# A Mamba block with a mixture of experts on one core: the next chunk's front part moved one unit sooner

## The reference

```
xz = u @ in_proj_w.T;  x_in, z = split(xz, 2)          # 256 channels each
xc = silu(causal_conv4(x_in) + conv_b)
dt, Bm, Cm = split(xc @ x_proj_w.T, [8, 24])
delta = softplus(dt @ dt_w.T + dt_b)
dA  = exp(delta * A)                                   # 16 states n for each channel
dBu = delta * Bm * xc
h = dA_t * h + dBu_t;   y = sum_n h * C_t              # over the time steps
y = (y + xc * D) * silu(z);  x = x + y @ out_w.T
# then x + silu(gate) * val @ ffp_w.T, then + sum over the top 2 of 8 experts
```

## Time and profile before

| | us |
|---|---|
| median of 3 runs | 856.88 |
| lowest and highest | 855.81, 859.95 |
| the profiled execution | 856.53 |
| its span from first to last instruction | 854.7 |
| DVE busy | 744.2 |
| PE busy | 655.0 |
| POOL busy | 583.4 |
| ACT busy | 498.0 |

### The profile page before, as it was taken

One profiled execution on the slowest core, in us unless ns is written; L12 is line 12 of the kernel. 1 busy time (PEld: TensorE's weight loads), 2 busy tenths in 40 slices (PEclk: granted clock), 3 DMA queues, 4 the chain that ended last, 5 costly groups with the idle time before them and its releaser, 6 DMA issues.

```text
span 854.7 us, 12652 instructions
## 1 busy us (share of the span) xinstructions
PE 655.0 (77%) x3573; PEld 472.6 (55%) x3573; DVE 744.2 (87%) x1147; ACT 498.0 (58%) x1071; POOL 583.4 (68%) x487
## 2 busy tenths in 40 slices
PE   4538688888677787897788687887785689987991
PEld 2224454455355446773477446763584457787991
DVE  1286999999999999999999999999999987785675
ACT  2545796876778576555756576556743664432440
POOL 1085676777966896788958985789758973455452
PEclk9659899999979988997989997997886689997996
DMA  7823234223313336543553246432635320122248
GB/s 177 268 89 102 87 112 124 77 82 117 113 55 101 100 103 203 151 125 94 179 160 131 97 116 206 129 109 99 187 108 164 126 86 20 45 57 70 61 126 236
DMA packets 81785, 102.31 MB, mean 120 GB/s; under 512 B 10344, under 2 KB 48948, under 8 KB 81700
## 3 DMA queue, kind: packets, MB, share of 16 engines
q1 hardware_dynamic: 77395, 92.58, 36.3%
q0 software_dynamic: 4320, 8.92, 2.9%
HBM read 89.93 MB, written 15.35 MB: 123 GB/s over the span
## 4 chain that ended last, share of the span: by engine, by line
DVE 36%; PE 33%; issue 19%; ACT 7%; SPq 2%; DMA 2%; POOL 1%; DVEq 1%; ACTq 0%; POOLq 0%
DVE state L1059 19%; DVE product L1069 5%; PE y L1270 4%; PE work_front L1230 3%; PE up L1383 2%; PE gate L1376 2%; PE y L1266 2%; PE up L1394 2%; PE work_front L1236 2%; DVE stats L989 2%; ACT decay L923 2%; PE gate L1295 1%; SPq L701 1%; PE up L1295 1%; DVE arena L1034 1%
## 5 line engine op out<-in xcount | busy, mean ns | idle before, releaser
L800 POOL TENSOR_TENSOR inflow<-du,b_wide 128x1024 f32<-128x1024 f32 x128 | 315.4, 2468 | 143.7 <-DVE product L1069 94.2
L1059 DVE TENSOR_TENSOR_SCAN state<-decay,carry,inflow 128x512 f32<-128x512 f32 x192 | 234.7, 1264 | 6.2 <-ACT decay L923 5.4
L1069 DVE TENSOR_TENSOR product<-state,c_wide 128x1024 f32<-128x1024 f32 (+1 forms) x98 | 149.8, 1528 | 3.7 <-PE y L1266 2.5
L1266 PE MATMUL y<-ident,product 128*128 128x128 f32 x704 | 111.9, 304 | 33.6 <-DVE product L1069 33.5
L1266 PEld LDWEIGHTS y<-ident,product 128*128 128x128 f32 x704 | 92.2, 158 | 76.3 <-DVE product L1069 41.1
L923 ACT ACTIVATE decay<-delta_odd,a_neg 128x512 f32<-128x512 f32 x128 | 86.5, 688 | 66.7 <-DVE state L1059 65.6
L830 POOL DMA_INDIRECT y_dram<-y_rows,x_rows x71 | 82.7, 1165 | 58.9 <-ACT y_rows L979 51.5
L923 ACT ACTIVATE decay<-arena,a_neg 128x512 f32<-128x512 f32 x128 | 86.3, 687 | 56.9 <-DVE state L1059 50.0
L1270 PE MATMUL y<-h_rows,ident 128*128 128x512 f32 x160 | 90.7, 660 | 7.7 <-ACT h_rows L888 7.1
L824 POOL DMA_INDIRECT row_dram<-m_tok,place x64 | 73.9, 1154 | 24.2 <-issue 14.3
L1059 DVE TENSOR_TENSOR_SCAN state<-decay,inflow 128x512 f32<-128x512 f32 x64 | 74.4, 1202 | 5.7 <-POOL inflow L800 2.5
(11 more groups left out here) (234 smaller groups left out, 1323.6 us busy)
## 6 DMA issues: line engine op xcount, KB each, us to landing
b_wide<-bc_dram SPq DMA_DIRECT2D x128, 256.0 KB
c_wide<-bc_dram SPq DMA_DIRECT2D x98, 256.0 KB
w_stage<-gate_up_dram SPq DMA_DIRECT2D x29, 344.0 KB, 4.3
x_rows<-row_dram SPq DMA_DIRECT2D x71, 65.0 KB, 2.9
arena<-gate_up_dram SPq DMA_DIRECT2D x8, 344.0 KB
x_tok<-in_x SPq DMA_DIRECT2D x8, 256.0 KB, 6.1
out<-x_tok SPq DMA_DIRECT2D x8, 256.0 KB
inflow<-y_dram SPq DMA_DIRECT2D x6, 256.0 KB, 3.1
```

Of the source, the lines that this page charges most:

```text
L800: e.tensor_tensor(inflow[:, key % 3], du[:, c % 2], b_wide[:, key % ROW_SLOTS:key % ROW_SLOTS + 1, :].to_broadcast([P, HALVES, CHUNK]), AL ...
L1059: e.tensor_tensor_scan(state[:, key % STATE_SLOTS, h, :], decay_bank[h][:], inflow[:, key % 3, h, :], 0.0 if c % (SEQ // CHUNK) == 0 else ...
L1069: e.tensor_tensor(product[:, key % 2, :, :wide], state[:, key % STATE_SLOTS, :, :wide], c_wide[:, key % ROW_SLOTS:key % ROW_SLOTS + 1, :wi ...
L1266: t = e.matmul(y_bank[r][:, y_at(s, h)], product[:, key % 2, h, s * P:(s + 1) * P], ident[:], is_transpose=True, start=n == 0 and s % 2 + ...
```

## The change

Two numbers in `plan`. A second front row is taken in unit 4 of chunk 0 too, so every later row comes one unit sooner; and the rows of the chunk after the next begin at unit 12, not 13. Before, rows 0, 1, 2 of the list run in units 13, 14, 15 and row 3 in unit 0 of the next chunk; now rows 0 to 3 run in units 12 to 15. Row 3 holds `u_tok`, `u_turn`, `u_t`, `halo` and `in0a`. `log_dt` goes from unit 9 to unit 8, and `series`, `small`, `log1p` from unit 10 to 9. No instruction is added or taken away.

```diff
-EARLY_FRONT = (1, 2, 3)
+EARLY_FRONT = (1, 2, 3, 4)
@@
         if i in EARLY_FRONT:
             put_all(*take_front(c + 1, 1))
-        front = take_front(c + (1 if n < D_STATE - 3 else 2), 1)
+        front = take_front(c + (1 if n < D_STATE - 4 else 2), 1)
         if n == 0 and c:
```

## The result

| | before | after |
|---|---|---|
| median, us | 856.55 of 4 runs | 875.20 of 4 runs |
| lowest and highest | 855.81, 859.95 | 873.13, 878.71 |
| the profiled execution | 856.53 | 878.71 |
| its span | 854.7 | 876.9 |

The ratio of after to before is 1.0214, with a 95% interval of 1.0181 to 1.0246: 18.65 us slower by the medians, where 14.1 over the median was forecast. The profiled execution of after is the highest of its four and 3.5 us over their median. So what it shows is partly what this one execution did. Its mean granted clock of TensorE (0.859) isn't lower than that of the other three (0.858, 0.853, 0.851); where its 3.5 us come from isn't shown.

The account below looks back on a forecast made before the run. The prediction took DVE to bound the unit loop, busy 71.1 of 74.4 us. It summed 856.5 + 11.1 (passages) + 3.3 (port), nothing for the softplus, to 870.9, said 871.0, with 860 to 881 to hold 8 in 10.

Parts of the forecast that it names:

- not more than 2 us each: Sign of error: stretches of the later chunks, without such a passage, moving by more than 2 us each.
- The chain, 13.4: Ends of chunks 0, 1, 2: ACT and PE steps from unit 14's scan end to `y_gate` sum to 13.4 us.
- S: End of unit 14's scan; taken to shift by -0.2 us in chunk 0 and -0.7 each in chunks 1 and 2.
- 5.7, 3.5 and 3.5: How much later, in us, `y_gate` comes after S at the ends of chunks 0, 1 and 2.
- Rival C: Slower: at the passages PE idles, then runs `in0a` and the totals at low clock; 881 us, chance 0.17.
- Part 2: Port between DVE and POOL: moved DVE steps meet or escape POOL's `inflow`; +3.3 us in sum.
- The 1.5 that it took off: Units 14 and 15, three chunks: `picked` finds POOL free (-0.8), the choice meets an `inflow` (+0.3); -1.5 us.
- the lock on the port: Unit 14, chunks 1 and 2: by the skill's exclusive lock the second choice step is held up 2.2; sum 0.7 more.
- Part 3: Softplus on ACT: `log_dt`, moved from unit 9 to 8, holds the next decays back by 4.8 but stays covered; nothing taken.
- 11.1, 3.3 and 0: Forecast terms in us: passages out of chunks 0 to 2, port between DVE and POOL, softplus on ACT.
- a DVE operation with two operands in SBUF: At the DVE/POOL port: such an operation that meets an `inflow` waits for its end.

## Why the prediction was right, and where it was off

**The mechanism and its place were right.** DVE waits ahead of `y_gate` at the ends of chunks 0, 1 and 2 and at no later one, for the sums of L1270, with L1230 ahead of them, and putting the crossing row back takes all but 0.2 of these waits and 11.8 us away. The stretches of the later chunks moved by 1.2, 1.3, 0.8, 1.4 and -2.0, about the "not more than 2 us each" that was asked.

**The chain, 13.4.** In the profile of after it is 16.9, 16.9 and 14.3, and as a reading of that profile the term is too small by 3.5, 3.5 and 0.9. The first passage shows why. Over the sum come the two waits of ACT for the turns (0.74 + 1.72) and the longer `in0a` (3.66 - 1.98 = 1.68). Off it comes 0.85: the sum had 1.98 for both totals ahead of `y_gate`, which began 1.13 after them (131.75 against 130.62). That is 3.3 of the 3.5. With the full clock, in the run with `rstd3` sooner, ACT waits only 0.44, and 13.4 + 0.44 - 0.85 = 13.0 is the distance there; the 3.9 between the two is the low clock. So the sum was right within 0.4 for the clock that it assumed, with two small errors that partly cancel, and `u_turn` hides beside the decays there but for the 0.44. The forecast should have given the chain two prices and a chance to each, instead of one price and a rival.

Measured by itself the crossing costs 12.8 ± 3.7 us against 12.7, and that the two agree so closely is luck. DVE alone doesn't need 9.9 after S at the second and third passages but 11.6: `picked` is held up as before, and a second routing step now is as well. By the trace the crossing added 6.8, 2.4 and 2.7 and not 5.7, 3.5 and 3.5.

**Rival C** came in part: in the profiled execution of after `in0a` ran at the low clock at the first two passages and not at the third (1.98). The Trainium skill (page TensorE: Matmul & The Clock Gate, Part 1) has an idle TensorE go back to 1.2 GHz. The traces agree in that the low clock of the first passage comes behind 2.51 us of idle time, and they add that the same 2.5 us, ahead of the same instruction, ended once in the low clock and once not.

**S.** Taken as 1.6 sooner over three chunks. In chunk 0 S is 0.2 later (114.87 against 114.69), though the first scan began 1.3 earlier in this execution (45.5 against 46.8), so 1.5; from `y_gate` to the next S it is 0.5 longer and 1.1 shorter. That is 0.9 later in all, so this term was off by 2.5. The gain in units 12 and 13 came in both chunks, by 2.4 and 3.0. What the sum lacked is what stands ahead of them: from `y_gate` to the end of unit 11 chunks 1 and 2 are 2.9 and 2.0 longer, 1.15 of it the held-up shift of unit 11 in each.

**Part 2, the port, +3.3.** The hold-up of the shift is there (1.27, forecast "about 1.3"), and it was counted for chunks 3 to 6 only, though chunks 1 and 2 have it too: in each of chunks 1 to 6 unit 11 is about 1.1 shorter once it is gone. The two tests of it gave 5.4 ± 3.7 and, with the clock's share in it, 9.3 ± 4.3. The sum's 4.8 is near the first, though its count of chunks was too small. The 1.5 that it took off came and more: `picked` is free in unit 15 of chunks 3 to 5, and these units are 1.4 to 1.5 shorter. It had no term for `series` in unit 9, held up to 2.55 in chunks 5 and 6 where it took 1.30. In unit 14 of chunks 1 and 2 the second choice step is held up, which the prediction named beside its sum as what the lock on the port would do:

```profile
197.00 2.36 DVE L1135 TENSOR_TENSOR both<-choice 128x32 f32<-128x32 f32 x1
```

It took 0.19 before. `x_one` begins 3.2 after S in both chunks, between the 2.95 of the sum and the 3.3 named there.

**Part 3, "I take nothing".** For `log_dt` this held, in chunk 0 too. It holds the next decays back by 4.8 there (from 92.42 to 97.23, with two table loads of 1.28), and the scan that needs them, unit 10's, has no idle time ahead of it; only `small` waits 0.59 for the result. The larger new waits of chunk 0 have a cause that the forecast doesn't have. In unit 6 half of the multiplication by C is given away, and `dt0`, which stood behind the turns of that unit on PE, now stands ahead of them. It waits 1.40 for `x_dbl`, a total behind it takes 1.92 for two matmuls (1.02 at full clock), ACT waits 2.90 for the turns, and `pre_dt0` and the decays of unit 8 come behind; their scan waits 1.46. The version with the softplus alone moved, where `dt0` keeps its place, has no wait in unit 8 (it has 1.60 in unit 9). By the profile the three waits are 2.5 us; the run that keeps chunk 0 as it was found no difference, so what they are worth in the end is open.

**The total.** Against 18.3 (1.0214 of 857): about 12 for the passages (11.8 and 12.8, from two pairs of versions), 5 for the hold-up at the port, and about 1 left over, which isn't told from nothing. The forecast had 11.1, 3.3 and 0. The 3.9 that it lacks are of the size of what S (2.5 in the profiled execution) and the port (5 against 3.3) lack; these two overlap, since the held-up shift of chunks 1 and 2 is in both, so this is an attribution by size and not a measurement.

## What to carry to other kernels

Work that crosses the end of a stage is priced by the chain that ends the stage, not by its engine's load: `in0a` is 2 us of PE in a loop that DVE bounds, and it lengthened a wait of DVE at each of the three passages. Where two engines share a port, a pause on one is a place for the other's steps; before a step on either side is moved, lay both timelines beside each other and ask who stands in the pause now, since the same edit won 5 or more in one order of the work and lost 13.6 in another. A step that waits for its input also delays what is queued behind it, on its own engine and on those that this feeds: `dt0` did that in unit 6 of chunk 0. And compare a sum with an execution at its clock: when a chain runs through TensorE behind a wait, price it at both clocks.

## What the runs showed that was not expected

- The granted clock at one place of the program differs between executions: 0.70 and 1.00 around the first passage, with the same instructions and the same idle times (2.51 and 2.50) ahead of them. It moved `y_gate` by 3.9 us after S.
- The clock can fall on a path that was free: at the passage from chunk 4 to 5 one kernel has 0.70 and eight matmuls of the totals at 1.95 us, another 1.00 and 1.07, after the same 1.69 us of idle time.
- A DVE step with one input was held up too: `small` (L1034, one operand in SBUF) took 2.65 beside an `inflow` and 0.69 in the pause. The prediction's words, "a DVE operation with two operands in SBUF", were too narrow; the earlier trace rows already had the case.
- POOL pays as well: two `inflow`s take 4.67 in a row, and 5.64 where a DVE step (`series`, or `delta`) that waited for the first gets in ahead of the second (2.35 and then 3.33).
- `picked` stays held up in chunks 1 and 2: it takes 2.4 in after as before, and the choice step ahead of it now takes 2.36.
